# Attention scores as one float32 product per head, on one Trainium2 core

## The reference

```python
q_hk  = (layernorm(x) @ Wq.T).reshape(B, S, H, K)        # S = 112, K = 128
q_big = einsum('bshk,hkq->bshq', q_hk, w_kc_q)           # q = 384 (rotary in layer 0)
q_r   = einsum('bshq,hqr->bhsr', q_big, W_qr)            # r = 64
k_r   = einsum('bld,hdr->bhlr', kv_rope, W_kr)           # l = 375, r = 64
scores = einsum('bhsr,bhlr->bhsl', q_r, k_r)
attn   = softmax(scores, axis=-1)
ctx_c  = einsum('bhsl,bld->bhsd', attn, kv_rope)
out    = (ctx_c through w_kc_kv, all heads side by side) @ Wo.T
```

## Time and profile before

| | before |
|---|---|
| median of 3 runs | 1052.57 us |
| profiled execution | 1053.55 us |
| its span, first to last instruction | 1051.8 us |
| TensorE busy | 965.4 us |
| VectorE busy | 665.3 us |
| ScalarE busy | 529.5 us |
| GpSimd busy | 515.0 us |
| mean granted TensorE clock | 0.981 of full speed |

### The profile page before, as it was taken

The page is one execution under the profiler, slowest core; times in us unless marked ns, Lnnn a source line. Parts: engine busy times, 40 slices in busy tenths (PEclk is TensorE's granted clock), DMA queues, the critical chain, the costliest instruction groups (busy, mean ns, idle before and its releaser), DMA issues. The chain is left out here.

```text
span 1051.8 us, 19586 instructions
## 1 busy us (share of the span) xinstructions
PE 965.4 (92%) x6132; PEld 566.5 (54%) x6141; DVE 665.3 (63%) x1180; ACT 529.5 (50%) x1238; POOL 515.0 (49%) x650
## 2 busy tenths in 40 slices
PE   3679999999999998899997799999999979989998
PEld 1335555556555555444343457677777654444443
DVE  5788778787877877398577547666666653322012
ACT  2255666576666666200475257777777762116400
POOL 4577777677777768111234056666666651100000
PEclk9899999999999999899999799999999999999999
DMA  8213223232322211451100022222012004104001
GB/s 242 70 44 108 84 68 105 54 112 62 117 65 85 62 45 42 161 187 55 46 36 31 30 71 72 71 70 62 15 62 70 0 1 192 38 1 169 0 31 40
DMA packets 30344, 75.56 MB, mean 72 GB/s; under 512 B 4967, under 2 KB 11239, under 8 KB 28126
## 3 DMA queue, kind: packets, MB, share of 16 engines
q1 hardware_dynamic: 24706, 66.31, 19.9%
q10 hardware_dynamic: 5596, 8.70, 3.0%
HBM read 63.98 MB, written 3.68 MB: 64 GB/s over the span
## 5 line engine op out<-in xcount | busy, mean ns | idle before, releaser
L1176 POOL TENSOR_SCALAR scratch<-scratch,rinv 112x375 f32<-112x375 f32 x256 | 154.9, 618 | 138.4 <-DVE rinv L1026 138.4
L897 ACT ACTIVATE scratch<-ps,mxn 112x375 f32<-112x375 f32 x256 | 144.3, 571 | 36.9 <-DVE mxn L1021 35.4
L1021 DVE TENSOR_REDUCE mxn<-ps 112x2 f32<-112x750 f32 x128 | 119.7, 935 | 41.9 <-PE ps L708 41.4
L762 PE MATMUL ps<-xnT,scratch 128*128 128x448 f16 x576 | 125.4, 365 | 8.4 <-DVE scratch L1100 4.1
L1157 POOL TENSOR_TENSOR scratch<-scratch 128x448 f32<-128x448 f32 x64 | 110.7, 1739 | 43.9 <-DVE scratch L1044 26.5
L749 PE MATMUL ps<-scratch,kvn_hi 125*128 125x224 f16 x768 | 119.9, 260 | 5.3 <-DVE scratch L1066 2.3
L1168 POOL TENSOR_TENSOR scratch<-scratch 128x375 f16<-128x375 f32 x128 | 115.5, 902 | 10.9
L734 PEld LDWEIGHTS ps<-ident,scratch 112*125 112x125 f32 x768 | 100.8, 188 | 35.4 <-issue 26.7
L734 PE MATMUL ps<-ident,scratch 112*125 112x112 f32 x768 | 105.4, 273 | 9.2 <-DVE scratch L1089 9.1
L1089 DVE TENSOR_TENSOR scratch<-ps,scratch 125x672 f16<-125x672 f32 x128 | 108.7, 850 | 4.9 <-ACT scratch L907 4.9
L1044 DVE TENSOR_TENSOR scratch<-ps,ropeq 128x448 f32<-128x448 f32 x192 | 110.0, 616 | 2.4 <-PE ps L762 2.0
(11 more groups left out here) (166 smaller groups left out, 1482.8 us busy)
## 6 DMA issues: line engine op xcount, KB each, us to landing
scratch<-in_wq SPq DMA_DIRECT2D x16, 512.0 KB, 4.4
scratch<-in_wo SPq DMA_DIRECT2D x16, 512.0 KB, 3.6
wabs<-in_w ACTq DMA_DIRECT2D x32, 256.0 KB, 3.0
scratch<-in_w SPq DMA_DIRECT2D x8, 1024.0 KB, 4.9
scratch<-in_W SPq DMA_DIRECT2D x8, 1024.0 KB, 6.1
scratch<-scratch SPq DMA_DIRECT2D x64, 112.0 KB, 2.2
scratch<-in_kcq SPq DMA_DIRECT2D x8, 512.0 KB, 3.4
scratch<-in_qr SPq DMA_DIRECT2D x32, 128.0 KB, 3.5
```

The lines of the kernel that those rows point to most:

```text
L762: last = nc.tensor.matmul(out, lhs[i](c), rhs[j](c), start=(n == 0), stop=(n == 3 * chunks - 1))
L897: last = nc.scalar.activation(prob[0:S, s % 2, hh, :], scores_ps[0:S, hh, 0:L], ACT.Exp, bias=mxn[0:S, s % 2, hh:hh + 1], accum_out=rsum[0 ...
L1021: nc.vector.tensor_reduce(mxn[0:S, s % 2, :], scores_ps[0:S, :, 0:L], AX_X, ALU.max, negate=True).then_inc(max_done, 1)
L1176: last = nc.gpsimd.tensor_scalar(prob[0:S, s % 2, hh, :], prob[0:S, s % 2, hh, :], rinv[0:S, s % 2, hh:hh + 1], P_SCALE, ALU.mult, ALU.mult)
```

## The change

The scores become one product per head with float32 operands. `qr` (float32, one tile) takes the place of `qr_hi` and `qr_lo`, and the keys are read from `kr` as ScalarE writes them; `kr_hi` and `kr_lo` are gone. The kinds C and Q leave `SPLIT_KINDS`: ScalarE has nothing to do for them, and VectorE copies them out with their scale in one operation. GpSimd's `keys_split` is gone. The scores wait for `k_out`; the key copy waits until the scores that read its buffer are done. The semaphores' start values are adapted to the groups that are left.

```diff
-SPLIT_KINDS = ("A", "C", "U", "M", "Q", "R")
+SPLIT_KINDS = ("A", "U", "M", "R")
...
-        kr_hi, a = view(scratch, a, [2, LPAD], F16)
-        kr_lo, a = view(scratch, a, [2, LPAD], F16)
...
-        qr_hi, a = view(scratch, a, [B, P], F16)
-        qr_lo, a = view(scratch, a, [B, P], F16)
+        qr, a = view(scratch, a, [B, P], F32)
...
-                if kind in ("C", "Q"):
-                    half = slice(n * B // 2, (n + 1) * B // 2)
-                    return (src[:, 0:HALF].rearrange("p (b n) -> p b n", b=B // 2),
-                            qr_hi[:, half, 0:S], qr_lo[:, half, 0:S], c_scale)
...
-                        pe.wait_ge(k_ready, nth(p, B, s))
+                        pe.wait_ge(k_out, nth(p, B, s))
...
-                        for i, (a, b) in enumerate(((qr_hi, kr_hi), (qr_hi, kr_lo), (qr_lo, kr_hi))):
-                            for hh in range(2):
-                                rows = slice(hh * R, (hh + 1) * R)
-                                last = nc.tensor.matmul(scores_ps[:, hh, 0:L], a[rows, s, :],
-                                                        b[rows, s % 2, 0:L],
-                                                        start=(i == 0), stop=(i == 2))
+                        for hh in range(2):
+                            rows = slice(hh * R, (hh + 1) * R)
+                            last = nc.tensor.matmul(scores_ps[:, hh, 0:L], qr[rows, s, :],
+                                                    kr[rows, s % 2, 0:L], start=True, stop=True)
...
-                            act.wait_ge(k_ready, nth(q, B, b - 2))
+                            act.wait_ge(scores_done, nth(q, B, b - 2))
...
-                                .then_inc(group_high, counts(p, g))
+                                .then_inc(group_high, 1)
...
-                    act.sem_inc(group_high, sum(g in split_order for g in order[:N_AHEAD]))
+                    if layer == 0:
+                        act.sem_inc(group_high, sum(g in split_order for g in order[:N_AHEAD]))
...
+                        if kind in ("C", "Q"):
+                            half = slice(n * B // 2, (n + 1) * B // 2)
+                            nc.vector.tensor_scalar(
+                                qr[:, half, 0:S], bank(p, g)[:, 0:HALF]
+                                .rearrange("p (b n) -> p b n", b=B // 2), c_scale, None,
+                                ALU.mult).then_inc(group_out, counts(p, g))
...
-                    def keys_split(q, b):
-
-                        pool.wait_ge(k_out, nth(q, B, b))
-                        pool.sem_inc(taken, 1)
-                        nc.gpsimd.tensor_copy(kr_hi[:, b % 2, 0:L], kr[:, b % 2, 0:L])\
-                            .then_inc(k_high, 1)
-                        pool.wait_ge(k_high, nth(q, B, b))
-                        nc.gpsimd.tensor_tensor(kr_lo[:, b % 2, 0:L], kr[:, b % 2, 0:L],
-                                                kr_hi[:, b % 2, 0:L],
-                                                ALU.subtract).then_inc(k_ready, 1)
...
-                                elif g[0] == "K" and runs(p, g):
-                                    keys_split(pair_of(p, g), g[1])
...
-                    nc.gpsimd.memset(qr_hi[:, :, S:P], 0.0)
-                    nc.gpsimd.memset(qr_lo[:, :, S:P], 0.0).then_inc(padded, 1)
+                    nc.gpsimd.memset(qr[:, :, S:P], 0.0).then_inc(padded, 1)
```

More of the change, by code:

```diff
@@ L527, in attention @@
             k_out = sem(f"{tag}_k_out")
-            k_high = sem(f"{tag}_k_high")
-            k_ready = sem(f"{tag}_k_ready")
             scores_done = sem(f"{tag}_scores_done")
```

## The result

The changed kernel takes 1077.07 us (median of 4 runs, 1074.65 to 1082.38) against 1052.3 (4 runs, 1051.37 to 1054.96), a ratio of 1.0238 with a 95% interval of 1.0194 to 1.0282. The profiled execution took 1078.21 us, its span is 1076.3. The prediction was 1073.5, slower with 0.89, and the time lies in its range. The sum that led there is right in its sign and nearly in its total, but two terms were too small, one that was booked at 0 costs 9 us, and one that the sum doesn't have gives as much back.

What follows compares the result with a forecast made beforehand. TensorE, 92% busy, was taken to bound the kernel. From a profiled 1053.55 us, +25.6 for products and -5 for the shorter chain gave 1074.2, or 1073.5 as a median; range 1063 to 1110 us.

Steps and rivals of the forecast that it cites:

- TensorE is the bound: Both attention stages: TensorE's own products set the time, so a microsecond added to a slot appears in the span.
- The 23.7 us of idle: All five attention stretches: the most TensorE idles there, busy 584.35 of 608 us.
- The products: Score products: two float32 products a slot take 0.78 us against 0.58, +0.20 in each of 128 slots, +25.6 us.
- 0.15 for entry and exit: Score group: 0.15 us for entering and leaving the split array, taken from group C, beside two steps of 0.315.
- loads might cost: Float32 weight loads before the scores: if the second head's first load follows the first's, +0.39 a slot, +50 us.
- The chain: Groups C and Q go straight to VectorE without ScalarE's copy, shortening TensorE's waits: 5 us back, between 0 and 6.3.
- GpSimd's work is off the path: GpSimd's casts and subtractions of the keys: 180.5 us of work removed, nothing on TensorE waits for them, booked 0.
- The new wait of the key copy: ScalarE's key copy waits until scores of the same buffer are read; always met when reached, so 0.
- VectorE's copy: Groups C and Q: a scaled copy from PSUM replaces a subtraction of the same shape, 0 within 0.3 us over 32.
- The marks: Wrong if a layer 1 slot isn't longer, or if stretches outside attention move by more than 1 us.
- Rival 1: Score products: heads not, or only partly, side by side; +66 us to 1114, or +106 us to 1154; chance 0.12.
- rival 2: Score products: split rows take both records of a product in one step, group 0.47 us, total 1034; chance 0.07.
- Rival 3: Attention stages: shortened chains and GpSimd's relief remove all 23.7 us of TensorE's idle, total about 1055; chance 0.05.

Runs made afterwards that it cites:

- two hops: Changed kernel with ScalarE's float16 copy of C and Q put back into an unread tile, VectorE waiting for it; 1081.54 us, ratio 1.0286.
- key split kept: Changed kernel with GpSimd's cast and subtraction of the keys put back, though nothing on TensorE waits for the result; 1071.56 us, ratio 1.0189.
- unequal heads: Changed kernel in which the second head streams 188 of its 375 key columns in the score products; 1075.66 us.

## Why the prediction came out as it did

```
us, profiled spans               predicted   measured   from
score products, 128 slots          +25.6       +32      0.83 - 0.58 a slot
C and Q in one hop                  -5          -6.2    after against two hops (4.1 in regular slots)
waits filled by longer products      0          -9.2    what is left in the stages (6.8 in regular slots)
GpSimd's relief                      0          +9.2    after against key split kept
outside the attention stages         0          -1.3    first, middle and last part
sum                                +20.6       +24.5
```

The third row isn't measured by itself. Its 6.8 us in regular slots are the places named above; the other 2.4 lie where slots differ between kernels in any case, and what made them isn't shown.

- **TensorE is the bound, and a microsecond in a slot comes out in the span.** Right for most slots, wrong for five of sixteen. The 23.7 us of idle held waits that were set elsewhere, and time put in front of them came for nothing. The listing of idle time showed them small: 0.33 of the 0.40 at slot 6, and none for the 0.25 at slot 7, since the modelled ends of products cover them.
- **The products.** The layout was right: two records a product, two heads side by side, two steps. The mis-sized step is the "0.15 for entry and exit" taken over from group C: 0.20 here. Group C's first step is longer by 0.05, the load of 64 float32 columns; that of 128 columns adds 0.107. The prediction had seen that loads might cost and kept it as a bound. It left them out of the sum: 0.107 - 0.054 is 0.053 a slot, 6.8 us, and 6.4 us too little were booked.
- **The chain.** -5 against -6.2, right. The waits for the copy of C and Q are gone but for one of 1.0 us ahead of the first scores of layer 0.
- **GpSimd's work is off the path, so 0.** This is the step that failed. Nobody waited for the key split, but it set when GpSimd began its rotary additions, and these share something with some of VectorE's operations from SBUF. With the split gone the 2.1 us addition comes first, and VectorE's subtraction, on which group A waits, is held for it.
- **The new wait of the key copy, VectorE's copy, the memset:** 0, and no row shows otherwise.
- **The marks.** Both signs of being wrong came true. Two slots of layer 1 aren't longer, and that counts against the reasoning: time in front of a wait came for nothing. And the stretches outside attention moved by more than the 1 us that I allowed, in both directions, which was a poor mark, as they vary by more than that between kernels that are alike there. Slots were to be longer by an equal 0.2 us; they are longer by 0.25 and unequal.
- **Rivals.** Rival 1 falls by the unequal heads, rival 2 by a group of 0.83 us in two steps. Rival 3 had the right idea in a small measure: 15 us of waits were given back, by the chain and by filling, not by GpSimd.

That the time is so near to the 1073.5 is luck: -9.2 and +9.2, neither of them foreseen, cancel. The range, 1063 to 1110, would have held with either of them alone, at about 1068 or 1086. No kernel of this study beats the one before; the best with float32 scores and a full result, the one with the idle key split, is 1.9% slower.

## What to carry to other kernels

Removing work from an engine that nobody waits for moves everything behind it on that engine earlier; before booking 0, look at what it will now meet, above all long GpSimd operations beside long VectorE operations that read and write SBUF. Price a product by the time from its first record to the next group's, and take entry, steps and exposed loads as separate terms, scaled by the columns of each. When products in a full TensorE get longer, some of the time falls into waits that were already there: compare slot by slot, since the totals hide gains and losses that cancel.

## What was not expected of the hardware

- GpSimd's SBUF additions and two kinds of VectorE's operations from SBUF, the subtraction and the scaled copy to float16, ran one after the other, whole instructions at a time, whichever came first: 2.99 us for one of 1.20, and on the other side 4.15 for a pair of additions of 3.17. Operations of VectorE from PSUM ran beside them at 0.61, and the short reciprocal from SBUF at 0.15.
- A float32 product that follows other work has a first step longer by the load of its weights: 0.054 us for 64 columns, 0.094 for 112, 0.107 for 128.
- With split rows, the shorter product's second record began by 703.10 and the longer one's only after 703.22, although the shorter one comes later in the program. The Trainium skill, "TensorE: Matmul & The Clock Gate", in "What overlaps and what doesn't", says that products start and end strictly in program order. The windows of the unequal heads show otherwise, for the starts, for two halves of the array with unequal lengths. Whether a semaphore on the last product then also covers the other half was not tried.
